# Attention values masked on GpSimd and key sums taken on TensorE, inside a hybrid state-space, attention and expert block

## The reference

```python
x = x + ssm(layernorm(x))      # (8, 512, 128)
x = x + experts(layernorm(x))  # 8 experts of 128 -> 512 -> 128, all of them, mixed by weights
x = x + attn(layernorm(x))     # 16 heads of 8, own chunk of 10 and 25 keys to the left
x = x + experts(layernorm(x))

# ssm: inner 64, 8 states per channel, so 512 recurrences over time per sequence
state = decay_t * state + drive_t
y = sum(state * c_t, axis=-1) + D * x_t
# attn
scores = einsum('bhsd,bhtd->bhst', q * 8**-0.5, k) + mask
probs = softmax(scores);  out = einsum('bhst,bhtd->bhsd', probs, v) @ Wo.T + bo
# experts
h = silu(x @ w_gate) * (x @ w_up);  out = sum_e cw[e] * (h[e] @ w_down[e])
```

## Time and profile before

| what | value |
|---|---|
| median of 3 runs | 1539.36 us (1535.48 to 1539.65) |
| the profiled execution | 1539.28 us |
| its span, first to last instruction | 1537.5 us |
| mean granted TensorE clock | 0.977 |
| TensorE matmuls busy | 1428.3 us, 93% |
| VectorE busy | 1000.8 us, 65% |
| ScalarE busy | 791.9 us, 52% |
| GpSimd busy | 459.5 us, 30% |

### The profile page before, as it was taken

How to read it: one execution, slowest core, us unless ns; L and a number is a source line. 1 busy time by engine, 2 the same in 40 slices (tenths; PEclk the granted TensorE clock), 3 DMA queues, 4 the chain that set the end, 5 groups by cost and what they waited for, 6 DMA issues and landing times.

```text
span 1537.5 us, 27266 instructions
## 1 busy us (share of the span) xinstructions
PE 1428.3 (93%) x10580; PEld 1227.8 (80%) x10580; DVE 1000.8 (65%) x2317; ACT 791.9 (52%) x1114; POOL 459.5 (30%) x416
## 2 busy tenths in 40 slices
PE   5789957999999989999999899999999999999998
PEld 3577846887888878788788788887888888888887
DVE  5655636777587666866876577658756776486543
ACT  6462723855467445674656456465742555366321
POOL 4342253234232342223621354115512221141000
PEclk9999977999999999999999899999999999999999
DMA  5110142001601151014200520034004200420000
GB/s 171 45 47 23 55 139 45 15 16 49 155 1 36 45 141 25 2 43 151 45 8 10 169 47 22 1 129 83 28 1 132 44 1 2 138 38 2 1 7 8
DMA packets 82076, 81.57 MB, mean 53 GB/s; under 512 B 4748, under 2 KB 55948, under 8 KB 81948
## 3 DMA queue, kind: packets, MB, share of 16 engines
q1 hardware_dynamic: 74444, 64.92, 15.8%
q10 hardware_dynamic: 7504, 14.91, 2.7%
...
## 4 chain that ended last, share of the span: by engine, by line
PE 69%; DVE 11%; DMA 7%; issue 5%; ACT 5%; POOL 3%; SPq 1%; ACTq 0%; DVEq 0%; POOLq 0%
PE pd L994 23%; PE pg L270 7%; PE pu L270 6%; PE pg L272 6%; PE pg L271 6%; PE pu L271 6%; PE pu L272 6%; DMA arena<-bc_spread 3%; PE att_ps L676 3%; DVE h L1087 2%; PE att_ps L698 1%; DMA v_rows<-staged 1%; DVE x L1075 1%; DMA att_arena<-v_rows 1%; DVE att_arena L798 1%
## 5 line engine op out<-in xcount | busy, mean ns | idle before, releaser
L1049 ACT ACTIVATE h<-pg 128x512 f32<-128x512 f32 x512 | 304.0, 598 | 631.2 <-PE pg L272 620.6
L994 PEld LDWEIGHTS pd<-w_down,h 128*128 128x128 f32 x4096 | 513.7, 193 | 31.1 <-issue 3.9
L994 PE MATMUL pd<-w_down,h 128*128 128x128 f32 x4096 | 533.2, 279 | 1.1 <-DVE x L1075 1.1
L1087 DVE TENSOR_TENSOR h<-h,pu 128x512 f32<-128x512 f32 x512 | 344.0, 676 | 207.2 <-PE pu L272 206.1
L270 PE MATMUL pg<-ffn_x_hi,w_gate_hi 128*128 128x512 f32 x512 | 246.2, 481 | 5.4 <-ACT h L1049 3.9
L270 PE MATMUL pu<-ffn_x_hi,w_up_hi 128*128 128x512 f32 x512 | 208.2, 407 | 27.4 <-DVE h L1087 27.3
L271 PE MATMUL pu<-ffn_x_lo,w_up_hi 128*128 128x512 f32 x512 | 205.5, 401 | 0.0
L271 PE MATMUL pg<-ffn_x_lo,w_gate_hi 128*128 128x512 f32 x512 | 205.4, 401 | 0.0
L272 PE MATMUL pg<-ffn_x_hi,w_gate_lo 128*128 128x512 f32 x512 | 205.0, 400 | 0.0
L272 PE MATMUL pu<-ffn_x_hi,w_up_lo 128*128 128x512 f32 x512 | 204.8, 400 | 0.0
L899 POOL TENSOR_TENSOR att_arena<-att_arena 128x512 f32<-128x512 f32 (+1 forms) x72 | 73.8, 1025 | 352.9 <-DVE att_arena L789 352.9
...
## 6 DMA issues: line engine op xcount, KB each, us to landing
arena<-bc_spread ACTq DMA_DIRECT2D x56, 256.0 KB
...
qk_rows<-qk_parts SPq DMA_DIRECT2D x32, 256.0 KB, 3.0
q<-qk_rows SPq DMA_DIRECT2D x32, 256.0 KB, 3.7
k<-qk_rows SPq DMA_DIRECT2D x32, 256.0 KB, 4.7
...
arena<-in_x SPq DMA_DIRECT2D x8, 256.0 KB, 2.9
```

What stands on the lines that cost most here:

```text
L994: last = nc.tensor.matmul(pd[:, t * P:(t + 1) * P], h_b[:, d % NH, t * P:(t + 1) * P], wd[:, d % NCH, :], start=d % CPE == 0 and t == 0, s ...
L1049: nc.scalar.activation(h_b[:, c % NH, :], pg[c % 2][:, :], ACT.Silu).then_inc(gate_done, 1)
L1087: nc.vector.tensor_tensor(h, h, pu[d % 2][:, :], ALU.mult).then_inc(h_done, 1)
```

## The change

- Values: VectorE writes v to `attT` in one copy; 256 KB go out to `v_rows` (now 128 wide), without zeros. Each of the four head positions gathers the same 128 columns, and GpSimd zeroes what is not its head's in the gathered windows (`like_heads`: parts of 4, 4, 4 and 5 windows, that is three multiplications of 128x1024 and one of 128x1280 a sequence). TensorE waits for these (`v_set`) in place of the DMAs. `clear_v` is gone, and GpSimd's queries no longer wait for `v_out`.
- Sums over keys: the tile is transposed undivided; after a window's eight products with the values, eight more matmuls with `ones` put the sums beside them in the same bank; VectorE takes a reciprocal (128x64) and divides while reading the result (`divided`, 128x60). The reduction, the old reciprocal, the division of the full tile and ScalarE's copy are gone.
- Slots: sequence 2's state-space part 4 chunks earlier; sequences 3 to 7: `ln` one earlier, first two steps three later; attention units start half a chunk later, at a pace of 4.1 (4.0), the last sequence's 3.22 (3.25).

```diff
     if i == 1:
         return dict(ln=1.5, win=3.5, dt=6, k=(9, 12, 15, 18), y=23.5)
     if i == 2:
-        return dict(ln=30, win=32.5, dt=36, k=(40, 43, 46, 49), y=54.5)
+        return dict(ln=26, win=28.5, dt=32, k=(36, 39, 42, 45), y=50.5)
     o = NCH * (2 * i - 4)
-    return dict(ln=o - 8, win=o - 6.5, dt=o + 1, k=(o + 7, o + 13, o + 26, o + 32), y=o + 42)
+    return dict(ln=o + -9, win=o + -6.5, dt=o + 1, k=(o + 10, o + 16, o + 26, o + 32), y=o + 42)
 T_SSM = [_ssm_slots(i) for i in range(B)]
 T_ATT = [38 + 55 * b for b in range(B)]
-ATT_PACE = [3.3] + [4.0] * (B - 2) + [3.25]
+ATT_PACE = [3.3] + [4.1] * (B - 2) + [3.22]
 _COLS = {}
...
-        v_d = nc.dram_tensor("v_rows", (NKEY, L), F32, kind="Internal").ap()
+        v_d = nc.dram_tensor("v_rows", (NKEY, P), F32, kind="Internal").ap()
...
-                return T_ATT[j] + 13.5 + n * ATT_PACE[j]
+                return T_ATT[j] + 14 + n * ATT_PACE[j]
...
                         scores(n + 1)
                     yield at(n + 1 + 3 / 8)
                     if n in (0, NW // 4):
-                        pe.wait_ge(v_moved[n > 0], 16 * 8 * (j + 1))
+                        pe.wait_ge(v_set, 4 * j + (4 if n else 2))
                     name = ("o", j, n)
                     ps = ab.take(pe, name)
                     pe.wait_ge(p_t, NUNIT * j + n + 1)
@@ -695,9 +697,14 @@
                     for i, w in enumerate(UNITS[n]):
                         for v in range(2):
                             for g in range(4):
-                                last = nc.tensor.matmul(ps[32 * g:32 * g + 32, i * QW:(i + 1) * QW],
-                                                        v_w[:, w, v, 32 * g:32 * g + 32], pt[n % 2][:, i, g, v, :],
-                                                        start=(i, v) == (0, 0), stop=(w, v) == (UNITS[n][-1], 1))
+                                nc.tensor.matmul(ps[32 * g:32 * g + 32, i * QW:(i + 1) * QW],
+                                                 v_w[:, w, v, 32 * g:32 * g + 32], pt[n % 2][:, i, g, v, :],
+                                                 start=(i, v) == (0, 0), stop=False)
+                        for v in range(2):
+                            for g in range(4):
+                                last = nc.tensor.matmul(ps[32 * g:32 * g + 32, (2 + i) * QW:(3 + i) * QW], ones[:, :],
+                                                        pt[n % 2][:, i, g, v, :], start=False,
+                                                        stop=(w, v) == (UNITS[n][-1], 1))
                     ab.fill(last, name)
                 yield Att.end(j) + 2
                 ps = ab.take(pe, ("proj", j))
...
                                          bias=pk("b_" + v)).then_inc(qk_hi, 1)
-                for n in range(NUNIT + 1):
-                    if n >= 1:
-                        m, nw = n - 1, len(UNITS[n - 1])
-                        yield at(n + 1 / 2)
-                        if m == 0 and j:
-                            ab.wait(act, ("proj", j - 1))
-                        ab.wait(act, ("o", j, m))
-                        ps = ab.ps(("o", j, m))[:, 0:nw * QW].rearrange("p (w q) -> p w q", q=QW)
-                        nq = WQ if nw == 2 else QW
-                        to = attT[:, 2 * m * WQ:2 * m * WQ + nw * nq].rearrange("p (w q) -> p w q", q=nq)
-                        ab.free(nc.scalar.copy(to, ps[:, :, 0:nq]), ("o", j, m))
-                    if n < NUNIT:
-                        yield at(n + 3 / 4)
-                        act.wait_ge(s_sub, NUNIT * j + n + 1)
-                        u = s_u[n % 2][:, 0:len(UNITS[n]), :, :]
-                        nc.scalar.activation(u, u, ACT.Exp, scale=float(HD) ** -0.5).then_inc(s_exp, 1)
+                for n in range(NUNIT):
+                    yield at(n + 3 / 4)
+                    act.wait_ge(s_sub, NUNIT * j + n + 1)
+                    u = s_u[n % 2][:, 0:len(UNITS[n]), :, :]
+                    nc.scalar.activation(u, u, ACT.Exp, scale=float(HD) ** -0.5).then_inc(s_exp, 1)
             @staticmethod
             def dve(dve, link, j):
...
-                dve.wait_ge(v_zero, j + 1)
                 if j == 0:
                     dve.wait_ge(v_pad, 32)
-                for t in range(TT):
-                    for r in range(4):
-                        ins = nc.vector.tensor_copy(v_s[:, t, r, :].rearrange("p (g h d) -> p g h d", g=4, d=HD)[:, :, r, :],
-                                                    ab.ps(("v", j))[:, t * P:(t + 1) * P]
-                                                    .rearrange("p (g h d) -> p g h d", g=4, d=HD)[:, :, r, :])
-                        if (t, r) == (TT - 1, 3):
-                            ab.free(ins, ("v", j))
-                        else:
-                            link.count(ins)
+                ab.free(nc.vector.tensor_copy(attT[:, :], ab.ps(("v", j))[:, :]), ("v", j))
                 def masked(n):
                     nw = len(UNITS[n])
...
                     nw = len(UNITS[n])
-                    u, s, rs = s_u[n % 2][:, 0:nw, :, :], ssum[:, 0:nw, :], rsum[:, 0:nw, :]
+                    u = s_u[n % 2][:, 0:nw, :, :]
                     dve.wait_ge(s_exp, NUNIT * j + n + 1)
-                    link(nc.vector.reduce_sum(s, u, AX))
-                    link(nc.vector.reciprocal(rs, s))
-                    link(nc.vector.tensor_tensor(u, u, rs.unsqueeze(3).broadcast_to([P, nw, 4, WK]), ALU.mult))
                     if n >= 2:
                         ab.wait(dve, ("o", j, n - 2))
                     nc.vector.transpose(pt_flat[:, n % 2, 0:nw * 4 * WK],
                                         u.rearrange("p w g k -> p (w g k)")).then_inc(p_t, 1)
+                def divided(n):
+                    nw, name = len(UNITS[n]), ("o", j, n)
+                    nq = WQ if nw == 2 else QW
+                    ab.wait(dve, name)
+                    link(nc.vector.reciprocal(rsum[:, 0:nw * QW], ab.ps(name)[:, 2 * QW:(2 + nw) * QW]))
+                    ps, rs = (a.rearrange("p (w q) -> p w q", q=QW)[:, :, 0:nq]
+                              for a in (ab.ps(name)[:, 0:nw * QW], rsum[:, 0:nw * QW]))
+                    to = attT[:, 2 * n * WQ:2 * n * WQ + nw * nq].rearrange("p (w q) -> p w q", q=nq)
+                    ab.free(nc.vector.tensor_tensor(to, ps, rs, ALU.mult), name)
                 for n in range(NUNIT + 1):
                     if n:
...
+                    if n:
+                        yield at(n + 5 / 8)
+                        divided(n - 1)
                 yield Att.end(j) + 2.5
                 ab.wait(dve, ("proj", j))
                 dve.wait_ge(x2_bias, j + 1)
...
                 ab.wait_free(sp, ("v", j))
-                sp.dma_start(v_d[LEFT:LEFT + L, :].rearrange("(t p) x -> p t x", p=P), u_b[:, :, :]).then_inc(v_out, 16)
+                sp.dma_start(v_d[LEFT:LEFT + L, :].rearrange("(t p) x -> p t x", p=P),
+                             attT.rearrange("p (t x) -> p t x", t=TT)).then_inc(v_out, 16)
                 for half_w, (w0, w1) in enumerate(((0, NW // 2), (NW // 2, NW))):
                     if half_w == 0:
...
-                            cols = v_d[w0 * WQ + 32 * v:w0 * WQ + 32 * v + 1, P * r:P * (r + 1)]
+                            cols = v_d[w0 * WQ + 32 * v:w0 * WQ + 32 * v + 1, :]
-                                                 ap=[[L, 32], [WQ * L, w1 - w0], [1, P]])).then_inc(v_moved[half_w], 16)
+                                                 ap=[[P, 32], [WQ * P, w1 - w0], [1, P]])).then_inc(v_moved[half_w], 16)
...
-                ab.wait_free(pool, ("v", j))
-                pool.wait_ge(v_out, 16 * (j + 1))
+                if j == 0:
+                    pool.wait_ge(w_small, 2)
...
+                def like_heads(part):
+                    w0, w1 = ((0, 4), (4, 8), (8, 12), (12, NW))[part]
+                    v = v_w[:, w0:w1, :, :].rearrange("p w j (g r d) -> p (w j g) r d", g=4, r=4)
+                    pool.wait_ge(v_moved[part // 2], 16 * 8 * (j + 1))
+                    nc.gpsimd.tensor_tensor(v, v, pk("head").unsqueeze(1).unsqueeze(3)
+                                            .broadcast_to([P, (w1 - w0) * 8, 4, HD]), ALU.mult).then_inc(v_set, 1)
...
+                        yield Att.at(j, n + 3 / 4 + part % 2 / 8)
+                        like_heads(part)
-            sp.dma_start(v_d[0:LEFT, :], u_b[0:LEFT, 0, :]).then_inc(v_pad, 16)
-            sp.dma_start(v_d[LEFT + L:NKEY, :], u_b[0:NKEY - LEFT - L, 0, :]).then_inc(v_pad, 16)
...
+                nc.gpsimd.memset(attT[0:32, 0:P], 0.0).then_inc(v_zero, 1)
+                pool.wait_ge(v_zero, 1)
+                nc.gpsimd.memset(ones[:, :], 0.0).then_inc(pads_set, 1)
+                pool.wait_ge(pads_set, 2)
+                for r in range(4):
+                    nc.gpsimd.memset(ones[32 * r:32 * r + 32, HD * r:HD * (r + 1)], 1.0).then_inc(pads_set, 1)
+                pool.wait_ge(pads_set, 6)
-                def clear_v(pool, link, j):
```

(8 more changed lines are left out.)

14 lines of the change are left out of this document (9 added, 5 removed).

## The result

| | before | changed |
|---|---|---|
| median | 1538.38 us (1534.95 to 1541.96, 8 runs) | 1531.28 us (1529.96 to 1533.26, 8 runs) |
| span of the profiled execution | 1537.5 us | 1529.0 us |
| mean granted TensorE clock | 0.977 | 0.984 |

The ratio is 0.9954, with a 95% interval of 0.994 to 0.9969: about 7 us less, where 17 were forecast. The direction was right, but under half of the gain came, and the experiments show that most single terms of the sum were off, in both directions.

What follows compares the result with a forecast made beforehand. TensorE, busy 1428.3 of 1537.5 us, was taken to bound the kernel. Terms gained 38.1 us and paid 20.7, net -17.4 from 1539.28, giving 1522 us, range 1500 to 1545.

Steps and rivals of the forecast that it cites:

- they have room: GpSimd's masks, 74 us in all, fit its 459.5 us of work in 1537.5 and were priced at nothing.
- the other slots: Slot moves besides sequence 2's steps: work shifts by a chunk or three in places without a wait, worth nothing.
- VectorE's relief: Division and reduction leave VectorE, shortening TensorE's waits for it after 262 us: 5 us gained, bounds 0 and 18.8.
- Sums on TensorE: Eight more matmuls in each of 136 windows, 0.13 us each group, on the path: 17.7 us paid.
- The rival of a whole visit each: Added sum matmuls cost a full visit's price again: 27.0 us in place of 17.7, giving 1531; chance 0.1.
- Queries without the wait for v: Attention 2 and 4: idle and slow clock of 17.6 us go, 5 return, 12.6 gained; gathered-value waits shrink by 1.
- next in line: After v, queries wait for q and k transfers, then c: 3 us return at attention 2, 2 at attention 4.
- Slots: Sequence 2's steps four chunks earlier: 36 us of loss at attention 0 goes, 16.5 comes in its place, 19.5 gained.
- The load: Sequence 2's input load waits for sequence 1's y matmuls, so VectorE and TensorE stand near 131 us: 3 us lost.
- The rival of the spreading queue: Spreads on two of sixteen DMA engines bind, so stalls at attention 0, 2 and 4 stay: 1554; chance 0.12.

Runs made afterwards that it cites:

- sums_twice: Changed kernel with each window's eight matmuls for the sums issued twice into the same place: 1544.21 us, 13 us more than the changed kernel.
- relief_only: Kernel before without VectorE's sum over keys, reciprocal and division, nothing in their place: 1519.25 us, ratio 0.988.
- values_only: Kernel before with the values' part alone (v without zeros, masks on GpSimd, queries without the wait): 1545.12 us, ratio 1.0045.
- quick spreads: Each spread of two broadcast rows made as two DMAs of one row, each to 64 partitions; on the kernel before, with nothing else, 1492.19 us.
- nomask_spread16: Kernel before with quick spreads and the values' part, but without GpSimd's head masks (output wrong): 1490.36 us, ratio 0.9686.
- before_spread16: Kernel before with each two-row spread made as two one-row DMAs, each to 64 partitions: 1492.19 us, ratio 0.9695.
- slots_only: Kernel before with the new slots alone: 1539.88 us, ratio 1.0007.

## Why the prediction was wrong

The step that failed most is the price of nothing for the masks on GpSimd ("they have room"): they cost 16 to 19 us. With it failed the price of nothing for the other slots, by some 12 us, and VectorE's relief was set at 5 us and measured 18. One by one, in the order of the prediction:

*Sums on TensorE, +17.7.* Nearly right as time on TensorE: 0.15 us a group in place of 0.13, 20.4 us. What the whole kernel pays for such groups is less, 13 us (`sums_twice`). The rival of a whole visit each (27.0) was wrong.

*VectorE, -5.* Mis-sized: 18 us (`relief_only`). I had capped it at the 18.8 us of waits after 262 us and then taken a quarter. It left out attention 0, where VectorE's unit work competes too and 8.0 us of the lead of `relief_only` arise by chunk 64, and the slow clock, some 3 us. After chunk 64 TensorE is idle 9.3 us less, half of the 18.8 and not a quarter. The list of waits hides this in the changed kernel, where `h` still shows 12.7 us; without the masks the total behind `h` after 60 us is 20.4 in place of 24.7, so part of what the relief took away came back by them.

*Queries without the wait for v, -12.6 and -1.* No run has it alone with slow spreads; in `values_only` 7.4 of the 11.3 us behind queries went, and as that part cost 7 us and the masks cost 16 to 19 in two other kernels, the remainder is an estimated gain of 9 to 12. The size was about right, but one step of it failed: at attention 4 I let 2 us come back, and put the queries' wait down to v, with q and k "next in line". k, and then the gathered values, came late, both slowed by the spreads, and 7.7 us are lost there. With quick spreads the wait for v costs hardly anything, and its removal with narrow rows gives little (`nomask_spread16` 0.9686, `before_spread16` 0.9695).

*Masking on GpSimd, 0.* The main failure: "they have room". GpSimd had room, but its instructions hold VectorE's off. Cost 16 to 19 us, in the trace with quick spreads 11.3 of waiting and 8.1 of slow clock. At one place, chunks 123 to 125, the hold is followed from instruction to clock; for the other places it is the likely cause, not a shown one. I bounded it by GpSimd's queue alone, though the trace of before held a sign that I had not looked for: the same four normalisations take 1.11 us in one place and over 3 in another.

*Slots, -19.5.* At attention 0 the gain was about as forecast: 15.6 us by chunk 64 in `slots_only`. But that the other slots "move work by a chunk or three in places without a wait: nothing" failed; it is given back at the later attentions, 9.0 us of it between chunks 192 and 208, net 0 alone and some 4 us gained beside the other parts.

*The load, +3.* VectorE did wait for it, 3.86 us, but the `h` behind it was hardly late: TensorE stood 0.20 and 0.55 us. Under 1 us.

So three terms carry the error: masks 16 to 19 us dearer, slots some 12 dearer (-16.5 with the load, measured -4), relief 13 better. Their sum is more than the 10 us by which the gain fell short, and need not equal it: alone the parts measured +7, +1 and -3, which is +5, and together -7. They share the same few waits, so what one term is worth depends on the others; a sum of separate terms, as I made it, can't hold that. That 1522 came as near as it did is luck: errors of both signs.

The rival of the spreading queue named the real cause of most of the stalls, at attention 0 and in sequence 1 and, by slowing v and k, at attention 2 and 4, but I let it decide only whether they would go. As a forecast of 1554 it was wrong: GpSimd's two multiplications a step waited 57.8 us in all for the spreads, not more than the 80.6 of before. As the place to look it was worth 47 us, and the that I had read (a DMA share of 0.11 in a stage that waits for DMA) showed it.

Open: why the new slots lose at attention 3; and how the masks' price divides between the hold on VectorE and their place in GpSimd's queue. The 8 to 9 us that moving them returned are no measure of the 16 to 19, which come from two other kernels, without the sums' part or with slow spreads.
